# First layer of a two-layer graph network: which engine's queue issues the loads of the sorted rows

## The reference

```python
# layer 0: mean of the neighbours' features, by SOURCE of the edge
agg = segment_sum(x[dst], src) / (count(src) + 1e-6)
x = layernorm(x + relu(concat([x, agg]) @ W + b))
# layer 1: graph attention with edge attributes and self loops
loop_attr = segment_sum(edge_attr, dst) / max(count(dst), 1)
s = leaky_relu(x_l[src] + x_r[dst] + edge_attr @ W_e)
alpha = softmax over the edges of a node of (s . att)
out = segment_sum(x_l[src] * alpha, dst) + bias
x = layernorm(x + out)
```

## Time and profile before

| | before |
|---|---|
| median of 3 runs (lowest, highest) | 1609.33 us (1607.97, 1613.49) |
| the profiled execution, its own time | 1610.33 us |
| its span in the profile | 1608.5 us |
| PE matmul busy | 1221.8 us (76%) |
| DVE busy | 1002.4 us (62%) |
| ACT busy | 771.1 us (48%) |
| POOL busy | 970.2 us (60%) |

### The profile page before, as it was taken

The page is one execution under the profiler, slowest core; times in us unless marked ns, Lnnn a source line. Parts: engine busy times, 40 slices in busy tenths (PEclk is TensorE's granted clock), DMA queues, the critical chain, the costliest instruction groups (busy, mean ns, idle before and its releaser), DMA issues. The chain is left out here.

```text
span 1608.5 us, 35020 instructions
## 1 busy us (share of the span) xinstructions
PE 1221.8 (76%) x8692; PEld 1083.7 (67%) x8702; DVE 1002.4 (62%) x2116; ACT 771.1 (48%) x2046; POOL 970.2 (60%) x970
## 2 busy tenths in 40 slices
PE   4887866888887778776797787888878887878650
PEld 2685856877777667765564777777777877777640
DVE  5333324644554444455654588888888878888858
ACT  0375644444455545410144665665655656556311
POOL 3277777777677766740001777777777777777501
PEclk9999889998999998988998899998999989999855
DMA  2233335555555555544101433333333333332001
GB/s 67 73 114 93 105 106 151 140 145 147 144 145 148 150 140 149 149 113 109 40 12 55 134 97 96 95 97 88 95 92 92 96 91 90 87 93 83 26 1 40
DMA packets 235701, 160.30 MB, mean 100 GB/s; under 512 B 29816, under 2 KB 220622, under 8 KB 235580
## 3 DMA queue, kind: packets, MB, share of 16 engines
q1 hardware_dynamic: 206396, 100.85, 24.1%
q0 software_dynamic: 29184, 58.01, 11.9%
HBM read 127.10 MB, written 34.39 MB: 100 GB/s over the span
## 5 line engine op out<-in xcount | busy, mean ns | idle before, releaser
L390 POOL DMA_INDIRECT sorted_rows<-row,place_idx x456 | 468.8, 1028 | 230.8 <-issue 173.5
L1134 POOL DMA_INDIRECT xl<-xl_rows,index_c x456 | 468.8, 1028 | 158.0 <-issue 132.5
L428 ACT COPY onehot_t<-ps_t 128x500 f32<-128x500 f32 x114 | 65.6, 575 | 284.2 <-PE ps_t L735 274.9
L1410 PE MATMUL ps_cs<-w_e,attr_t 128*125 128x128 f32 x912 | 193.9, 298 | 3.7 <-DVE work_c L1324 3.1
L1411 PE MATMUL ps_cs<-src_sum,onehot_ct 128*125 x912 | 191.3, 295 | 0.0
L601 DVE TENSOR_TENSOR away_s<-row_in,pair_bucket 128x4 f32<-128x4 f32 x135 | 21.9, 162 | 223.3 <-DMA row_in<-sorted_rows 215.9
L1410 PEld LDWEIGHTS ps_cs<-w_e,attr_t 128*125 128x125 f32 x912 | 155.4, 213 | 4.2 <-issue 3.3
L746 PE MATMUL ps_g<-row_in,onehot_s 128*128 128x129 f32 x976 | 143.9, 295 | 18.2 <-DVE onehot_s L606 18.2
L1411 PEld LDWEIGHTS ps_cs<-src_sum,onehot_ct 128*125 128x125 f32 x912 | 153.2, 210 | 0.0
L746 PEld LDWEIGHTS ps_g<-row_in,onehot_s 128*128 128x128 f32 x976 | 131.9, 210 | 24.6 <-issue 22.5
L1148 ACT ACTIVATE apart<-column,dst_lo 125x128 f32<-125x128 f32 x456 | 145.6, 394 | 4.6 <-PEq L858 4.6
(11 more groups left out here) (307 smaller groups left out, 2385.8 us busy)
## 6 DMA issues: line engine op xcount, KB each, us to landing
row_in<-sorted_rows SPq DMA_DIRECT2D x540, 66.0 KB
attr<-in_ea SPq DMA_DIRECT2D x456, 62.5 KB
attr_c<-in_ea SPq DMA_DIRECT2D x456, 62.5 KB
sorted_rows<-row,place_idx POOLq DMA_INDIRECT x456
xl<-xl_rows,index_c POOLq DMA_INDIRECT x456, 3.3
xl_rows<-x_nodes SPq DMA_DIRECT2D x5, 320.0 KB, 2.5
out<-x SPq DMA_DIRECT2D x4, 320.0 KB
sorted_rows<-x SPq DMA_DIRECT2D x5, 66.0 KB, 2.0
```

The lines of the kernel that those rows point to most:

```text
L390: pool.indirect_dma_start(out=m.sorted_rows.rearrange("k p w -> (k p) w"), out_offset=bass.IndirectOffsetOnAxis(ap=m.place_idx[:, k:k + 1] ...
L1134: pool.indirect_dma_start(out=xl[x][:, u, :], out_offset=None, in_=m.xl_rows, in_offset=bass.IndirectOffsetOnAxis(ap=index[half][:, b * U ...
L1410: pe.matmul(out, attr_t[off % 2][:, u, :], m.w_e[:], start=True, stop=False)
```

## The change

`load_rows` is taken out of SP's program and put into ACT's. ACT issues a group after its row copy of step j when `when[q] - 1 <= j`; SP issued it after the attribute loads of index j when `when[q] + 2 <= j`. The waits in `load_rows` are the same, on ACT instead of SP. ACT's loop runs to `END + 2` as SP's did.

```diff
@@ sync
-            def load_rows(q):
-                if q % G2 == 0:
-                    scattered(sp, ready[q // G2])
-                    sp.wait_ge(cleared, 16 * NP)
-                    sp.wait_ge(pairs_ready, q // G2 + 1)
-                if q >= B2:
-                    sp.wait_ge(src_summed, q - B2 + 1)
-                tiles = numbers(nc, sp, m.tile2_i, q * U, U, NP * T2 - 1)
-                for u in range(U):
-                    sp.dma_start(row_in[q % B2][:, u, :], m.sorted_rows[bass.ds(tiles[u], 1), :, :].rearrange(
-                        "o p w -> (o p) w")).then_inc(row_back[q % B2], 16)
-
             sp.wait_ge(numbers_ready, 1)
-            begun = 0
             for j in range(END + 2):
...
-                while begun < len(when) and when[begun] + 2 <= j:
-                    load_rows(begun)
-                    begun += 1
@@ scalar
-            for j in steps:
+            def load_rows(q):
+                if q % G2 == 0:
+                    scattered(act, ready[q // G2])
+                    act.wait_ge(cleared, 16 * NP)
+                    act.wait_ge(pairs_ready, q // G2 + 1)
+                if q >= B2:
+                    act.wait_ge(src_summed, q - B2 + 1)
+                tiles = numbers(nc, act, m.tile2_i, q * U, U, NP * T2 - 1)
+                for u in range(U):
+                    act.dma_start(row_in[q % B2][:, u, :], m.sorted_rows[bass.ds(tiles[u], 1), :, :].rearrange(
+                        "o p w -> (o p) w")).then_inc(row_back[q % B2], 16)
+
+            begun = 0
+            for j in range(END + 2):
...
                     act.copy(row[j % B][0:TE, :, 0:P], ps_x[0:TE, :].rearrange("p (u d) -> p u d", u=U)).then_inc(
                         row_copied, 1)
+                while begun < len(when) and when[begun] - 1 <= j:
+                    load_rows(begun)
+                    begun += 1
```

## The result

| | before | changed |
|---|---|---|
| median | 1611.22 us | 1723.99 us |
| lowest, highest | 1607.97, 1613.49 | 1716.76, 1735.14 |
| ratio, 95% interval | | 1.0692 [1.0665, 1.0719] |
| span of the profiled execution | 1608.5 us | 1714.9 us |

The change makes the kernel 7% slower: 113 us, against 22 forecast, and outside the range. The loss lies where it was looked for. Busy times by stretch of the changed kernel (columns as in the earlier trace rows): up to the first row groups, the steps with row groups, the last groups.

What follows compares the result with a forecast made beforehand. It took SP's sequencer as the bound (48 x 2.5 = 120 us in 21 steps). After the change, 123 x 80 / 21 = 469 plus 2 x 12 = 493 us against 470.5, +22: 1631 us, range 1570 to 1680.

Steps and rivals of the forecast that it cites:

- Rival B: On ACT's queue: a group costs more than on SP (dear register read or no overlap with copies); 1672 to 1705, chance 0.13.
- A round trip of two steps sets the pace: Steps with row groups: ACT issue, landing, DVE, PE turn, ACT copy, next issue; 10.0 us for two steps, kernel +22 us.
- Sum 10.0 us for two steps: Round trip from ACT's issue to its next: issue 2.5, landing 2.2, L601 to L428 3.3, L428 to hand-over 2.0.
- bookkeeping: Phases in two windows, bucket count and chunks of PE work, delaying PE's turn: estimated 12 us a window.
- The landing, "I take 2.2": From the end of a group's issue of four transfers to L601: 2.2 us, with 1.7 or 2.7 as alternatives.
- From L601 (629.04) to L428 (632.34) 3.3: Round trip from DVE's L601, through PE's sums and turn, to ACT's L428: 3.3 us, read from one step.
- The longest way, "115.5 us": 21 steps: two-group steps by ACT's order, the rest by round trips; three stretches of 17.0 and three of 21.5 us.
- Reads of numbers, "7.5 us in 21 steps": PE's reads every third step before the turn, waits in front of L735: 7.5 us in 21 steps, giving 123 us.
- The loss "in steps 43 to 54 and 64 to 75": Where the profile would show the loss, with row copies of blocks 33 and 113 about 490 us apart.
- Rival A: Steps with row groups: round trip shorter than thought, ACT's order holds; faster, 1584 us, at best 1549, chance 0.27.
- D: Transfers themselves are the limit, so who issues them doesn't matter; no change, 1609 us, chance 0.07.
- C: Two queues share the descriptor generator, so ACT's issues wait while SP issues; slower, 30 us, 1661 us, chance 0.13.

Runs made afterwards that it cites:

- the split: Kernel before, with every third row group issued by ACT three steps ahead, the others by SP as before: 1553.62 us, ratio 0.962.
- SP at ACT's moment: Kernel before, SP still issuing rows, but each group waits for ACT's row copy of the step before its use: 1723.13 us, ratio 1.0674.
- no attribute loads: Changed kernel without loads of edge attributes after the first six blocks (output differs): 1673.8 us in a single run.
- reads moved: Changed kernel, PE's tile-number reads moved behind the spread before the row groups, DVE's in front of the landing wait: 1677.85 us, ratio 1.0408.
- both: Changed kernel with register reads moved and no attribute loads after the first six blocks (output differs): 1631.45 us, ratio 1.0109.

## Why the prediction was wrong, point by point

- *SP's sequencer is the bound of the kernel before, POOL the next:* right, and shown by the split.
- *A group costs on ACT as on SP, 2.5 us; ACT's queue goes on while its engine works:* right. From one group's first issue to the next one's in the same step it is 2.37 us in the median and 2.5 in the mean, and the first issue comes 0.15 us after the copy's start (median). Rival B falls.
- *The steps before block 33 and the last window are unchanged:* right. The row copies of block 33 lie 0.9 us apart, and the last 27 groups take 66 us before and 64.5 after.
- *A round trip of two steps sets the pace, and the kernel gets slower:* right, shown from both sides (earlier issue takes the loss away, later issue on SP makes it).
- *"Sum 10.0 us for two steps"*: here the prediction failed. The loop was the right one, but the terms of its sum were too short. With its two-group steps, reads and bookkeeping the forecast comes to 12.3 us for two steps (493 / 40), and 14.5 were measured. For the 80 steps 493 us were forecast and 576 measured, 83 more. The trip by parts, averaged over the groups of steps 34 to 111 in each trace: from a row copy's start to the end of the last issue, from there to L601, from L601 to the L412 two steps on, from that to its row copy (us). The first line is an estimate of the same parts from the prediction's terms: 2.5 for each of 27 groups in 21 steps, and its reads (0.7) and bookkeeping (0.6) put into the third. It comes to 12.0 and not 12.3, since the prediction added up a longest way and not averages:

```
                        issue   landing   L601 to L412   to row copy   sum
forecast's terms         3.2      2.2         4.6            2.0       12.0
changed                  2.88     3.07        5.99           2.55      14.49
SP at ACT's moment       4.83     1.95        5.11           2.57      14.46
no attribute loads       2.88     1.88        6.15           2.51      13.43
reads moved              2.88     3.14        5.10           2.47      13.60
both                     2.80     1.98        5.26           2.37      12.42
```

  - *The landing, "I take 2.2".* It was 3.1. With 3.1 in the sum, a trip is 10.9 (13.4 from a two-group step), and 21 steps take 3 x 17.9 + 3 x 24.3 = 126.6 us instead of 118.5: 31 us. Rows of a kernel in which one queue issues both kinds of transfer in turn can't show what two queues in parallel do; the range of 1.7 to 2.7 was too narrow.
  - *"From L601 (629.04) to L428 (632.34) 3.3".* The prediction itself calls this the shortest form of that stretch, and took it for every trip. It is the shortest in the changed kernel too (3.30), but the average is 5.99. Even in the 25 steps with one group, no bookkeeping and no read it is 4.5 in the median. The reads and the bookkeeping priced beside it make 4.6, so 1.4 us a trip are missing here, more than at the landing. What lengthens the stretch beyond the reads stays open.
  - *The longest way, "115.5 us".* With my own numbers a four-step stretch is longer by two trips (12.5 + 10.0 = 22.5) than by 21.5: 3 us in 21 steps, 11 us.
  - *Reads of numbers, "7.5 us in 21 steps".* That is 29 us in 80 steps, for PE alone. DVE's reads stood behind its wait for rows and were not counted. Moving both gave 35, so the term was short by some 6 us (before that run I put them at 52).
  - The rest of the 83, 35 us, has no term of its own. The same sum for the kernel with both pieces removed (landing 1.8, no reads) gives about 462 us and 494.8 were measured, and for the kernels with only the reads moved and only the attribute loads removed it is 33 and 40 us short. So about the same amount is missing in all four; by the table most of it lies between L601 and L412. That the kernel with both removed comes out at the forecast's 1631 is therefore chance in part. PE's own speed is no more than a small part of it: its matmuls took 413 us instead of 374 for the same number in the changed kernel, at a granted clock of 0.85 instead of 0.92, but with both pieces removed the clock is back at 0.91 (240 to 700 us) and 33 us are missing still.
- *The loss "in steps 43 to 54 and 64 to 75":* wrong. These 24 steps lose 42 us of the 106. The 21 steps behind block 75, which have no bookkeeping, take 151.7 us instead of 125.6, where the forecast had no loss at all.
- *Rival A (the trip is short)* fell, *D (transfers are the limit)* too. *C* was right in that two queues hinder each other, wrong in where: the issue is not longer (339 ns on ACT with SP issuing beside it, 333 on SP before), the landing is. The rule quoted from the Trainium skill (Perfetto Trace Analysis, "DMA Instruction — HWDGE"), that the generator is locked for one issue, shows no price in these rows.
- The rule quoted from the Trainium skill (DMA: Bandwidth & Descriptors, "Issuing engines are not separate DMA queues") says that a second engine saves only the sequencer's time. The runs agree that this time is saved, but it isn't all: the landing grew as well. And the page calls that time "usually small relative to the DMA itself"; here it was 2.5 us a group against a landing of 2.0, and taking a third of the groups off SP was worth 62 us.

## What to carry to other kernels

Moving transfers to another engine's queue moves two things: the cost of the issue, and its place in that engine's order of waits. Here the second decided: with the issue one step before its use the kernel lost 7%, with three steps nothing. Before such a move, follow the loop from the issue through landing and use back to the next issue, count its steps, put every hidden piece on it at full price, and take each stretch at its average and not at its shortest; then issue so many steps ahead that the loop is shorter than the engines' own pace. And an overloaded queue needs only a part taken off: a third of the groups, three steps ahead, made the kernel 3.8% faster, while all of them at the same distance made no difference.

## What the runs showed of the hardware

- The landing of four transfers of 66 KB after the last issue (medians): 1.5 us in the last window, with no attribute loads beside them; 2.1 there when two queues issue such groups at once; in the steps, 1.7 without attribute loads, 2.0 when the same queue issues them in turn, 3.1 when another queue issues them at the same time.
- A read of four numbers into registers takes 0.31 us on ACT's queue and 0.55 on SP's (medians). The same read is 0.46 to 0.47 for SP's other table, so the engine is not all of the difference.
- ACT's queue runs ahead of its engine: the read of a group's numbers begins 0.3 us before the row copy that stands in front of it starts, and the first transfer 0.15 us after that start (medians of 81 steps).
- PE's mean granted clock, as a share of the upper of its two levels (1.2 and 2.4 GHz), and its busy share in the steps with row groups: 0.92 and 79% before, 0.85 and 72% in the changed kernel, 0.95 and 84% in the split one. The same matmuls took 374 us before and 413 in the changed kernel. That the waiting lowers the clock was not tested.
